# First four heads' parts stored ahead of the others; batch 1's third part spread over the lead's units of maxima

## The chip, the cores and the metric

The kernel runs on one core of a Trainium2 chip. The metric is device time in microseconds of the whole program, from its start to its end. One core has TensorE (matrix products), VectorE, ScalarE and GpSimd for elementwise work, SyncE which here only issues transfers, and 16 DMA engines that carry them. TensorE's weight loads and products are told apart in the rows as PEld and PE, the transfers issued by SyncE as SPq.

## What is computed

Four layers over x of 2 batches, 1024 tokens, 128 channels. Cut to their cores:

```python
x = _layernorm(x + retention(x))      # L0_attn: 8 heads, rotary, decayed causal scores, gate silu(g)
x = _layernorm(x + L0_ffn(x))         # below
x = _layernorm(x + attention16(x))    # L1_attn: 16 heads of 8, two masked corners
x = _layernorm(x + x @ (ternary(W) * scale).T)

def L0_ffn(x):
    x = x + mla_attention(rmsnorm(x))  # 16 heads of 8, causal
    return x + moe(rmsnorm(x))         # 4 experts, top 1

def mla_attention(x):
    q = x @ Wq.T                       # rotated
    latent = layernorm(x @ Wdkv.T)     # 64 wide
    k, v = latent @ Wuk.T, latent @ Wuv.T   # k rotated
    return softmax(causal(q @ k.T / sqrt(8))) @ v @ Wo.T
```

The change bears on the hand-over from the first layer, the retention, to `mla_attention`.

## The kernel before

Everything is written by hand: each engine has its own instruction stream, and counting semaphores join them. The rows of x are 16 tiles of 128 tokens, 8 for each batch.

**Retention** runs a loop over the 16 tiles, numbered 0 to 15, a few steps of each tile late. The norm, projections and rotation of `mla_attention` are done for groups of four tiles, which I call parts 0 to 3 (two for each batch). Parts 0 and 1 (batch 0) are made inside this loop. Part 2 and 3 (batch 1) are made later, part 2 at the place of this change. q and k of a part are split into three bf16 pieces, so that bf16 products give float32 accuracy, and stored to DRAM (`store_parts`, L1163) as seven copies in the order in which products need them. From there they are loaded again as *stacks*: one stack (`load_stack`, L1182) holds four heads, with (head dimension, piece) along the partitions, 56 rows for even heads and 56 for odd ones. The stored rows are 128 partitions: 16 heads of 8, so heads 0 to 3 are partitions 0 to 31. `store_parts(0, 0)` is called for batch 0 of the first attention; its first half of columns (part 0) is stored at 197 us, its second (part 1) as soon as the last piece is made.

**Attention** works on blocks m: a group of four heads and one half of the queries. For each block the row maxima of the scores are found first, in *units of maxima* `A (u, x)`: TensorE makes 128 queries by up to 512 keys for two heads into a pair of PSUM banks, VectorE reduces it. When a block's units are done, `M` transposes its maxima, ScalarE copies them and GpSimd's `split` cuts them in three bf16 pieces and sends them by three small transfers into the query stack. Only then can the block's scores `S (s, x)` be made on TensorE, already less their maxima; ScalarE takes exp of them and `V` multiplies by the values. Units of maxima run ahead of the scores by a *lead* of 8 to 12 units, so the first 8 units (steps -8 to -1) have no scores beside them.

**What sets the order.** `order()` builds one list of all steps from tables of (step, what), and each engine goes through the same list and takes its share of each entry. So a step that waits holds up all later entries of that engine. Steps whose PSUM is taken from the common ring (`RINGED`: A, M, T0, Q, QS, lat and others) get bank pairs alternately, banks 2 and 3, then 0 and 1; entry r waits until entry r-2 has been emptied. The steps at one number stand behind that number's units of maxima, the split last (L1123 sorts them so).

Names of this place:
- `D16a`, `D16b`, `D16c`, `D17a`, `D17b`: last steps of the retention's last tile, 15. On TensorE D16a is its gate product (L485), D16b the projection of tile 14 (L495), D16c the turn of tile 15 (L504), D17a the projection of tile 15 (L495). ScalarE's share of D17a is `affine` (L521, 8 instructions), VectorE's `gated` (L542).
- `hn`, `T0`, `Q`, `QS`, `lat`, `ls`, `q_rot` of part 2: scaling (ScalarE L447); transposes (TensorE L1494, copied by ScalarE L1782); the query product and its swapped twin (L1499, copied at L1788); the latent product (L1510, copied at L1799); the latent's statistics (VectorE L468 and L471) and after them the reciprocal root on GpSimd (`latents_rooted`, L453 and L383 to L387); the rotation of the queries (GpSimd L460 to L462).
- `ln3`: root of the last part's norm on GpSimd (L1318, then L383 to L434).
- `warm`: products into an unused bank, of 128x512 (L1427), whose result nobody reads.
- Units of maxima: products at L1477 and L1487, reductions at L1930 (two heads) and L1927 (narrow units). Scores: L1557 and L1566. M: L1529, its copy L1818. Split: L1331 to L1334, its transfers L1341.

## Time and profile before

| | |
|---|---|
| median of 3 runs | 1020.18 us (1018.56 to 1020.27) |
| profiled execution, its own time | 1024.54 us |
| its span, first to last instruction | 1022.1 us |
| TensorE's mean granted clock | 0.957 |
| busy: TensorE, VectorE, ScalarE, GpSimd | 87%, 75%, 64%, 38% |
| transfers | 52.51 MB, mean 51 GB/s |

All times in the rows are microseconds from the span's start, in this one execution. A row of the order of time gives start, duration, engine, line, operation, tiles and count; a merged row counts the instructions and its duration goes from the first to the last. What stands in brackets is how long the engine was idle before, and what released it. The chain of waits is followed back from the last instruction: at each step to what released it. PEclk is TensorE's granted clock: 1.00 is 2.4 GHz, 0.50 is 1.2 GHz.

### The profile page before, as it was taken

To read this page: it belongs to the slowest core of one execution; us is meant where nothing else is said; L and a number is where in the kernel's file an instruction comes from. 1 tells how busy PE (TensorE), PEld (TensorE's weight loads), DVE (VectorE), ACT (ScalarE), POOL (GpSimd) and SP (SyncE) were. 2 spreads that over 40 slices of the span, in tenths; PEclk is the share of its full clock that TensorE was granted. 3 is DMA by queue.
4 is the path that set the end of the run, shared out by engine and by line. 5 is a ranking of instruction groups with operands and counts; after the bars stand their busy time and mean duration, and the time that the engine had idled before them with its cause. 6 is when DMAs were issued, how large, how long until landed. Compare 5 with 4: busy or idle time off the path is not lost.

```text
span 1022.1 us, 22793 instructions
## 1 busy us (share of the span) xinstructions
PE 890.6 (87%) x9065; PEld 445.1 (44%) x9070; DVE 762.3 (75%) x1155; ACT 655.0 (64%) x1285; POOL 392.0 (38%) x607
## 2 busy tenths in 40 slices
PE   5999999998877889988798778879988999999983
PEld 3778677777632343333472322216422222222232
DVE  3667766856487678886458498776889999999954
ACT  2554655655526678774446547765767988898981
POOL 2755757878332552134345111352432111111240
PEclk8999999999899999997799899989999999999997
DMA  8000000200501034111420601032206100000000
GB/s 294 1 1 2 1 1 2 73 2 1 150 1 41 21 128 138 38 43 52 122 74 2 199 21 38 5 92 85 75 2 187 32 20 20 21 20 2 5 23 21
DMA packets 49405, 52.51 MB, mean 51 GB/s; under 512 B 8874, under 2 KB 40618, under 8 KB 49140
## 3 DMA queue, kind: packets, MB, share of 16 engines
q1 hardware_dynamic: 45012, 48.12, 15.5%
q0 software_dynamic: 4288, 2.94, 1.1%
q8 instruction: 72, 1.18, 0.5%
q14 instruction: 33, 0.27, 0.1%
HBM read 32.37 MB, written 19.68 MB: 51 GB/s over the span
## 4 chain that ended last, share of the span: by engine, by line
PE 50%; DVE 27%; ACT 7%; issue 6%; DMA 4%; POOL 3%; SPq 2%; another core or an unknown queue 1%; DVEq 0%; ACTq 0%; POOLq 0%
DVE arena L1930 19%; PE banks L1592 10%; PE banks L1557 7%; PE banks L1477 5%; ACT arena L1750 3%; PE banks L740 3%; PE banks L485 3%; PE banks L495 2%; PE banks L1667 2%; PE banks L1675 2%; PE banks L673 2%; DMA arena<-arena 1%; PE banks L735 1%; PE banks L699 1%; ACT arena L521 1%
## 5 line engine op out<-in xcount | busy, mean ns | idle before, releaser
L1930 DVE TENSOR_REDUCE arena<-banks 128x2 f32<-128x1024 f32 (+1 forms) x384 | 440.9, 1198 | 65.4 <-PE banks L1477 33.0
L1750 ACT ACTIVATE arena<-banks 128x512 f32<-128x512 f32 (+1 forms) x768 | 409.4, 587 | 120.9 <-PE banks L1557 77.7
L1592 PE MATMUL banks<-arena 128*9 128x256 f32 (+1 forms) x3328 | 257.0, 385 | 6.8 <-ACT arena L1763 4.6
L1557 PE MATMUL banks<-arena 61*128 61x512 bf16 (+4 forms) x896 | 167.5, 373 | 33.9 <-ACT arena L1750 23.7
L1477 PE MATMUL banks<-arena 56*128 56x512 bf16 (+3 forms) x896 | 165.2, 371 | 29.1 <-DVE arena L1930 22.1
L1557 PEld LDWEIGHTS banks<-arena 61*128 61x128 bf16 (+1 forms) x896 | 44.7, 93 | 194.5 <-ACT arena L1750 160.8
L1331 POOL CAST arena<-arena 16x128 bf16<-16x128 f32 x32 | 9.0, 282 | 301.0 <-ACT arena L1818 292.3
L1592 PEld LDWEIGHTS banks<-arena 128*9 128x9 f32 x3328 | 51.6, 89 | 133.0 <-issue 86.7
L1477 PEld LDWEIGHTS banks<-arena 56*128 56x128 bf16 x896 | 45.2, 95 | 54.6 <-DVE arena L1930 40.9
L383 POOL TENSOR_TENSOR arena<-arena 128x8 f32<-128x8 f32 (+1 forms) x35 | 51.3, 1466 | 30.2 <-DVE arena L2094 27.8
L1341 POOL DMA_DIRECT2D arena<-arena x96 | 55.2, 579 | 10.7 <-POOL arena L1334 9.2
L521 ACT ACTIVATE arena<-banks,arena 128x128 f32<-128x128 f32 x128 | 46.4, 477 | 0.5 <-PE banks L504 0.5
L1371 POOL DMA_INDIRECT expert_rows<-arena x22 | 21.4, 972 | 54.9 <-DVE arena L2026 54.9
L1927 DVE TENSOR_REDUCE arena<-banks 128x4 f32<-128x1024 f32 (+1 forms) x32 | 30.4, 954 | 16.2 <-PE banks L1487 13.5
L511 ACT ACTIVATE arena<-banks 128x1024 f32<-128x1024 f32 x16 | 16.4, 1022 | 39.9 <-PE banks L740 39.9
L554 DVE TENSOR_TENSOR arena<-banks,arena 128x128 f32<-128x128 f32 x16 | 4.7, 291 | 47.0 <-PE banks L495 47.0
L1746 ACT ACTIVATE arena<-banks 128x512 f32<-128x512 f32 (+1 forms) x64 | 27.9, 490 | 17.2 <-PE banks L1566 16.9
L529 ACT ACTIVATE arena<-banks 128x1024 f32<-128x1024 f32 x16 | 16.4, 1026 | 33.9 <-PE banks L485 32.5
L767 DVE TENSOR_TENSOR arena<-banks,arena 128x1024 f32<-128x1024 f32 x16 | 19.6, 1223 | 24.0 <-PE banks L673 23.9
L485 PE MATMUL banks<-arena 128*128 128x128 f32 x256 | 33.9, 287 | 2.6 <-DVE arena L770 2.6
L673 PE MATMUL banks<-arena 128*128 128x512 f32 x64 | 32.8, 637 | 1.7 <-DMA arena<-c_gk 1.7
L866 POOL TENSOR_TENSOR arena<-arena 128x512 f32<-128x512 f32 x16 | 25.3, 1578 | 22.5 <-DVE arena L770 22.5
(239 smaller groups left out, 1463.5 us busy)
## 6 DMA issues: line engine op xcount, KB each, us to landing
arena<-k_products SPq DMA_DIRECT2D x32, 224.0 KB
arena<-q_products SPq DMA_DIRECT2D x64, 112.0 KB
q_products<-arena SPq DMA_DIRECT2D x16, 384.0 KB, 3.3
k_products<-arena SPq DMA_DIRECT2D x16, 384.0 KB, 3.8
arena<-e_w SPq DMA_DIRECT2D x22, 256.0 KB
arena<-arena POOLq DMA_DIRECT2D x96, 4.0 KB, 1.7
sorted_rows<-c_pads SPq DMA_DIRECT2D x2, 709.5 KB, 8.6
arena<-sorted_rows SPq DMA_DIRECT2D x4, 258.0 KB, 3.1
```

Source lines behind the costliest of these rows:

```text
L383: link(eng.tensor_tensor(y, v, epst[:, 1:2].to_broadcast(list(v.shape)), ALU.pow))
L485: ins = nc.tensor.matmul(bank(s // 4)[:, (s % 4) * P:(s % 4 + 1) * P], wg[:, s * P:(s + 1) * P], XT[:, i, :], start=True, stop=True)
L521: ins = nc.scalar.activation(ga[:, s, :], bank(4 + s // 4)[:, (s % 4) * P:(s % 4 + 1) * P], ACT.Identity, scale=gn[:, 0, s:s + 1], bias=gn ...
L673: ins = nc.tensor.matmul(bank(c), XT[:, n + 1, :], wqk[:, c * 512:(c + 1) * 512], start=True, stop=True)
L740: ins = nc.tensor.matmul(bank(2 + s // 4)[:, (s % 4) * P:(s % 4 + 1) * P], sm[:, s, :], vv[n % 2][:, s, :], start=first, stop=True, skip_g ...
L1341: g_.dma_start(rows, nmp[k % 2][:, i, :]).then_inc(mrow[k % 2], 16)
L1477: ins = nc.tensor.matmul(bank(first + par)[:, at:at + hi - lo], Qs[k_][rows, qc, y, qo:qo + P], Ks[k_][rows, y, lo:hi], start=True, stop=n ...
L1557: ins = nc.tensor.matmul(bank(S_BANK + (use + par) % SCORES)[:, at:at + C - o], Ks[n % NS][rows, y, kt * P:(kt + 1) * P], Qs[n % NS][rows, ...
L1592: ins = nc.tensor.matmul(PS[h * VROWS:h * VROWS + VW, AV_BANK, o:end], V[:, b, kt, HG * g + h, :], Pr[u % PROBS][:, h, o:end], start=(kt = ...
L1750: s_.activation(Pr[s % PROBS][:, 2 * x + par, o:C], scores[:, o:C], ACT.Exp) \
L1927: v_.tensor_reduce(of, two_banks.rearrange("p r (y e) -> p r y e", y=2)[:, :, :, 0:width], AX.X, ALU.max).then_inc(ring_dve, 1)
L1930: v_.tensor_reduce(of[:, :, x], two_banks[:, :, 0:width], AX.X, ALU.max).then_inc(ring_dve, 1)
```

## The change

Two things. First, `store_parts` takes a range of partitions. For batch 0 of the first attention it is called for partitions 0 to 31 (heads 0 to 3) before the first stack is loaded, and for partitions 32 to 127 after it, ahead of the second stack's load. The counts that stored parts are waited for with go up by one group of transfers. Second, the steps of part 2 from T0 to q_rot, which all stood at step -9, ahead of the first unit of maxima, stand at steps -8 to -3, and `("warm", 6)` at step -7 is gone.

```diff
--- before.py
+++ after.py
@@ -415,7 +415,7 @@
         def stored_wait(eng, w, i):
 
             if i >= 2:
-                eng.wait_ge(part_stored[w][i % 2], 16 * PART_DMAS[w] * (i // 2))
+                eng.wait_ge(part_stored[w][i % 2], 16 * PART_DMAS[w] * (i // 2 + 1))
 
         def first_of(m):
 
@@ -1065,9 +1065,9 @@
 
         def batch1_projections():
 
-            at = [(-9, e) for e in (("D16a", 15), ("warm", 8), ("D16b", 15), ("hn", 2), ("T0", 2), ("D16c", 15), ("Q", 2), ("QS", 2), ("lat", 2),
-                                    ("ls", 2), ("q_rot", 2))]
-            at += [(-8, ("warm", 2)), (-7, ("warm", 6)), (-7, ("D17a", 15)), (-6, ("D17b", 15)), (-2, ("ln3", 3)),
+            at = [(-9, e) for e in (("D16a", 15), ("warm", 8), ("D16b", 15), ("hn", 2), ("D16c", 15))]
+            at += [(-8, ("T0", 2)), (-8, ("warm", 2)), (-7, ("D17a", 15)), (-7, ("Q", 2)), (-6, ("D17b", 15)), (-6, ("QS", 2)),
+                   (-5, ("lat", 2)), (-4, ("ls", 2)), (-3, ("q_rot", 2)), (-2, ("ln3", 3)),
                    (1, ("q_part0", 2)), (5, ("ln", 2)), (6, ("KL", 2)), (6, ("xs3", 3)), (6, ("q_rem", 2)), (7, ("K", 2)),
                    (7, ("q_part1", 2)), (8, ("KS", 2)), (8, ("k_rot", 2)), (8, ("q_part2", 2)), (9, ("V0", 2)),
                    (10, ("hn", 3)), (11, ("T0", 3)), (12, ("Q", 3)), (13, ("QS", 3)), (14, ("lat", 3)), (15, ("ls", 3)),
@@ -1160,7 +1160,7 @@
 
             @block.sync
             def _(sp):
-                def store_parts(l, b):
+                def store_parts(l, b, lanes=slice(0, P), turn=0):
                     for c in range(2):
                         cols = slice(c * C, (c + 1) * C)
                         item = l * 4 + 2 * b + c
@@ -1168,16 +1168,18 @@
 
                         sp.wait_ge(pj["q_part2"], item + 1)
                         for i in range(2):
-                            sp.dma_start(q_dram[l, b, :, 3 * i:3 * i + 3, cols],
-                                         q[:, i:i + 1, :].to_broadcast([P, 3, C])).then_inc(part_stored[0][c], 16)
-                        sp.dma_start(q_dram[l, b, :, 6:7, cols], q[:, 2:3, :]).then_inc(part_stored[0][c], 16)
+                            sp.dma_start(q_dram[l, b, lanes, 3 * i:3 * i + 3, cols],
+                                         q[lanes, i:i + 1, :].to_broadcast([lanes.stop - lanes.start, 3, C])) \
+                              .then_inc(part_stored[0][c], 16)
+                        sp.dma_start(q_dram[l, b, lanes, 6:7, cols], q[lanes, 2:3, :]).then_inc(part_stored[0][c], 16)
                         sp.wait_ge(pj["k_part2"], item + 1)
                         for i in range(2):
-                            sp.dma_start(k_dram[l, b, :, 3 * i:3 * i + 3, cols], k).then_inc(part_stored[1][c], 16)
-                        sp.dma_start(k_dram[l, b, :, 6:7, cols], k[:, 0:1, :]).then_inc(part_stored[1][c], 16)
+                            sp.dma_start(k_dram[l, b, lanes, 3 * i:3 * i + 3, cols], k[lanes]) \
+                              .then_inc(part_stored[1][c], 16)
+                        sp.dma_start(k_dram[l, b, lanes, 6:7, cols], k[lanes, 0:1, :]).then_inc(part_stored[1][c], 16)
                     for w in range(2):
                         for c in range(2):
-                            sp.wait_ge(part_stored[w][c], 16 * PART_DMAS[w] * (l * B + b + 1))
+                            sp.wait_ge(part_stored[w][c], 16 * PART_DMAS[w] * (l * B + b + 1 + (l + b + turn > 0)))
 
                 def load_stack(n, part):
                     l, b, g, k = n // (B * NG), n // NG % B, n % NG, n % NS
@@ -1254,12 +1256,13 @@
                     for i in range(W1S, SORTED):
                         load_w1(b, i, steer)
 
-                store_parts(0, 0)
+                store_parts(0, 0, slice(0, HG * AD))
                 sp.wait_ge(k_rotated, NTILE)
                 sp.wait_ge(rot_ready, NTILE)
                 sp.wait_ge(qkT_done, NTILE)
                 load_all(0)
                 load_ones(sp, 0)
+                store_parts(0, 0, slice(HG * AD, P), 1)
                 load_all(1)
                 load_ones(sp, 1)
                 sp.wait_ge(g_done, NTILE)
```

On **TensorE**, from the last tile's steps into the lead, before (L1494 is T0, L504 the turn of tile 15, L1499 Q and QS, L1510 lat, L1477 and L1487 a unit of maxima):

```order
L495 MATMUL banks<-arena 128x128 x8
L1494 MATMUL banks<-arena 128x128 x4
L504 MATMUL banks<-arena 128x128 x8
L1499 MATMUL banks<-arena 128x512 x2
L1510 MATMUL banks<-arena 128x64 x4
L1477 MATMUL banks<-arena 128x512 x2
L1487 MATMUL banks<-arena 128x64 x4
L1477 MATMUL banks<-arena 128x512 x2
L1487 MATMUL banks<-arena 128x64 x4
L1427 MATMUL banks<-arena 128x512 x2
L1477 MATMUL banks<-arena 128x384 x2
```

and now (lines are three higher: L1480 and L1490 are a unit, L1497 is T0, L1430 the fillers, L495 the projection of tile 15; Q, L1502, follows the last row shown):

```order
L495 MATMUL banks<-arena 128x128 x8
L504 MATMUL banks<-arena 128x128 x8
L1480 MATMUL banks<-arena 128x512 x2
L1490 MATMUL banks<-arena 128x64 x4
L1480 MATMUL banks<-arena 128x512 x2
L1490 MATMUL banks<-arena 128x64 x4
L1497 MATMUL banks<-arena 128x128 x4
L1430 MATMUL banks<-arena 128x512 x2
L1480 MATMUL banks<-arena 128x384 x2
L1490 MATMUL banks<-arena 128x64 x4
L1480 MATMUL banks<-arena 128x384 x2
L1490 MATMUL banks<-arena 128x64 x4
```

T0 went behind the first two units, Q behind the last tile's projection; QS and lat follow one unit each later.

On **ScalarE** at the same place, before (L1782 is T0's copy, L521 the affine, L1788 and L1799 the copies of Q, QS and lat, L1818 that of the maxima):

```order
L529 ACTIVATE arena<-banks 128x1024
L447 ACTIVATE arena<-arena 128x128 x4
L1782 ACTIVATE arena<-banks,arena 128x512
L1788 ACTIVATE arena<-banks 128x512 x2
L1799 ACTIVATE arena<-banks 128x256
L521 ACTIVATE arena<-banks,arena 128x128 x8
L1818 ACTIVATE arena<-banks 16x128
```

and now:

```order
L529 ACTIVATE arena<-banks 128x1024
L447 ACTIVATE arena<-arena 128x128 x4
L1785 ACTIVATE arena<-banks,arena 128x512
L521 ACTIVATE arena<-banks,arena 128x128 x8
L1791 ACTIVATE arena<-banks 128x512 x2
L1802 ACTIVATE arena<-banks 128x256
L1821 ACTIVATE arena<-banks 16x128
```

The affine of the last tile (the second L521) went ahead of the copies of Q, QS and lat; T0's copy still stands directly ahead of it.

On **GpSimd**, behind the latent's root, whose end is L387, before (L460 to L462 are q_rot, L1331 to L1341 the first split and its transfers, L1318 the start of ln3):

```order
L387 TENSOR_TENSOR arena<-arena 128x4
L460 TENSOR_TENSOR arena<-arena 128x512
L461 TENSOR_TENSOR arena<-arena 128x512
L462 TENSOR_TENSOR arena<-arena 128x512
L1331 CAST arena<-arena 16x128
L1332 TENSOR_TENSOR arena<-arena 16x128
L1333 CAST arena<-arena 16x128
L1334 TENSOR_TENSOR arena<-arena 16x128
L1341 DMA arena<-arena 2x8x128 x3
```

and now (L1334 to L1344 are the split, L1321 the start of ln3):

```order
L387 TENSOR_TENSOR arena<-arena 128x4
L1334 CAST arena<-arena 16x128
L1335 TENSOR_TENSOR arena<-arena 16x128
L1336 CAST arena<-arena 16x128
L1337 TENSOR_TENSOR arena<-arena 16x128
L1344 DMA arena<-arena 2x8x128 x3
L460 TENSOR_TENSOR arena<-arena 128x512
L461 TENSOR_TENSOR arena<-arena 128x512
L462 TENSOR_TENSOR arena<-arena 128x512
```

The root of part 2 now stands directly ahead of the first split, and q_rot between it and ln3. On VectorE the statistics (L468, L471) went from ahead of the first unit's reduction to behind A(4,1)'s.

## Rows read from the trace of the kernel before

**Rows 1.** Chain of waits, 255 to 320 us: start, duration, what.
```profile
264.85 3.51 DMA k_products<-arena
...
308.39 3.73 DMA arena<-arena
```

**Rows 2.** Busy time, PEclk, DMA share and GB/s, in stretches of 1 us.
```profile
265.00:266.00 1.00, 0.92 (x8) 0.92 (x9) 0.02 (x1) 0.88 (x1) 0.76 (x4) 1.00 0.97 337
...
272.00:273.00 1.00, 0.00 (x0) 0.00 (x0) 0.61 (x4) 1.00 (x4) 0.00 (x0) 1.00 0.97 215
...
280.00:281.00 1.00, 1.00 (x6) 1.00 (x6) 0.00 (x0) 0.00 (x0) 0.81 (x1) 0.50 0.00 0
...
282.00:283.00 1.00, 1.00 (x19) 0.80 (x17) 0.00 (x0) 0.00 (x0) 0.00 (x0) 1.00 0.00 0
```

**Rows 3.** Order of time, SyncE's queue: start, duration, engine, line, operation.
```profile
261.57 0.89 SPq L1171 DMA_DIRECT2D q_products<-arena  x2
```

**Rows 4.** Order of time, TensorE; in brackets the idle time before.
```profile
265.08 2.05 PE L495 MATMUL banks<-arena 128*128 128x128 f32 x16 [0.75 <-DVE arena L542]
267.45 0.63 PE L1494 MATMUL banks<-arena 128*128 128x128 f32 x4 [0.32 <-ACT arena L447]
...
268.95 1.96 PE L1499 MATMUL banks<-arena 128*128 128x512 f32 x4
270.74 1.10 PE L1510 MATMUL banks<-arena 128*128 128x64 f32 x8
273.98 0.39 PE L1477 MATMUL banks<-arena 56*128 56x512 bf16 x2 [2.14 <-DMA arena<-q_products]
...
277.42 2.74 PE L1427 MATMUL banks<-arena 128*128 128x512 bf16 x6
279.95 2.66 PE L495 MATMUL banks<-arena 128*128 128x128 f32 x16
...
282.99 1.04 PE L1427 MATMUL banks<-arena 128*128 128x512 bf16 x3
...
294.78 0.39 PE L1557 MATMUL banks<-arena 59*128 59x512 bf16 x2
```

**Rows 5.** Order of time, VectorE.
```profile
272.36 0.61 DVE L468 BATCH_NORM_STATS2 arena<-arena 128x6 f32<-128x64 f32 x4 [3.93 <-ACT arena L1799]
...
274.47 4.09 DVE L1930 TENSOR_REDUCE arena<-banks 128x2 f32<-128x1024 f32 x4 [1.08 <-PE banks L1487]
278.47 1.22 DVE L542 TENSOR_TENSOR arena<-arena 128x1024 f32<-128x1024 f32 x1
283.10 1.23 DVE L1927 TENSOR_REDUCE arena<-banks 128x4 f32<-128x1024 f32 x1 [3.42 <-PE banks L1487]
...
286.40 2.35 DVE L1930 TENSOR_REDUCE arena<-banks 128x2 f32<-128x1024 f32 x2
```

**Rows 6.** Order of time, ScalarE.
```profile
268.12 0.69 ACT L1782 ACTIVATE arena<-banks,arena 128x512 f32<-128x512 f32 x1 [0.81 <-PE banks L1494]
...
272.16 2.90 ACT L521 ACTIVATE arena<-banks,arena 128x128 f32<-128x128 f32 x8
```

**Rows 7.** Order of time, GpSimd.
```profile
273.47 0.23 POOL L453 TENSOR_SCALAR arena<-arena 128x4 f32<-128x4 f32 x1 [7.04 <-DVE arena L471]
...
275.76 0.20 POOL L387 TENSOR_TENSOR arena<-arena 128x4 f32<-128x4 f32 x1
...
278.61 2.20 POOL L462 TENSOR_TENSOR arena<-arena 128x512 f32<-128x512 f32 x1
288.32 0.28 POOL L1331 CAST arena<-arena 16x128 bf16<-16x128 f32 x1 [7.51 <-ACT arena L1818]
...
297.68 0.20 POOL L387 TENSOR_TENSOR arena<-arena 128x4 f32<-128x4 f32 x1
```

**Rows 8.** GpSimd's transfers of the first row of maxima, 286 to 300 us.
```profile
L1341 POOL DMA_DIRECT2D arena<-arena x3: 560/566/814, 290.2 to 291.6; - x3
...
DMA to landing us min/median/max: 1.7/1.7/1.9
```

## The prediction

> **What bounds the kernel now.** The change touches one place of the run: the hand-over from the retention phase to the attention lead, 260 to 312 us. I read the chain of waits first, then the order of time of each engine there. The chain shows which transfers are waited for: the last store of batch 0's parts, 3.51 us, and the last transfer of the second row of maxima, 3.73 us [rows 1]. SyncE's queue says why the first one is on the path: the stores of the second half start at 261.57 [rows 3], the last lands at 264.85 + 3.51 = 268.36, and only then may the load of the first stack be issued. TensorE waits for that stack 2.14 us and starts the first unit of maxima, A(0,0), at 273.98 [rows 4]. In the 2 to 10 us before it, TensorE, ScalarE and VectorE do T0, Q, QS, lat and ls of batch 1's third part, under cover of this transfer [rows 4 to 6]. From 274.47 on VectorE sets the pace with its reductions of about 1.17 us, but for a gap of 3.42 us before 283.10, where it waits for A(2,0) behind the last tile's projection [rows 4, 5]. S(0,0), the first product of scores, runs at 294.78 [rows 4]. It needs the row of maxima that GpSimd splits from 288.32 and whose last transfer is issued at 291.6 and lands 1.7 us later, at 293.3 [rows 7, 8]. So this row is there 1.5 us before it is wanted. Behind S(0,0) the run is one chain of equal steps to the end, and what S(0,0) loses or gains the end does.
>
> I follow four marks through the change: A(0,0) starts, A(2,0)'s reduction starts (283.10), A(4,1)'s reduction ends (286.40 + 2.35 = 288.75, [rows 5]), S(0,0) starts.
>
> **Part 1: the store of the first four heads goes ahead.** Of the 1.8 MB that goes out between 262.5 and 268, a quarter is left in front of the load. The stores move 337 GB/s while they run [rows 2], so the quarter is 1.3 us of transfer, less than its six issues take. Six issues of about 0.45 us (the first two took 0.89, [rows 3]) put the last at 263.8. From issue to landing such a store takes between 1.7 us (the smallest transfer here, [rows 8]) and 3.51 us (the last store, with a queue ahead of it, [rows 1]). I take 1.8, since little is queued: it lands at 265.6 instead of 268.36. The loads are the same, so A(0,0) comes **2.75 us earlier** (bounds 2.9 and 1.05), at 271.2. TensorE is free by then: the turn of the last tile ends near 268.8, since T0 no longer stands before it.
> One row speaks against the full rate: the load into 56 partitions at a time moves 215 GB/s where the store of 128 moves 337 [rows 2]. The Trainium skill, "SBUF — State Buffer", section "Door 1: The DMA port swizzle", says that partitions 0 to 31 reach 8 of the 16 ports; by it the quarter would move at about half the rate, an estimate of 2.7 us of transfer, and A(0,0) would come about 0.7 us later than I say. The trace has no transfer of 32 partitions.
> The rest of the store, 96 partitions of both halves, 12 issues and some 2.7 MB, now stands between the first and the second stack's load. At the same rate it is 8 us, to about 279, and the second stack is in by 285; it is first read by units of maxima behind S(0,0). Cost nothing. The waits raised by one DMA group in the later stores and copies are met long before.
>
> **Part 2: what moves into the lead.** The engines' work is the same but for 6 fillers less on TensorE (2.74 us at half clock, [rows 4]). What counts is the order in each queue.
> From A(0,0) to A(2,0) it was 283.10 - 273.98 = 9.12 us. Now T0 stands in the ring of bank pairs behind A(0,1) and takes A(0,0)'s pair, so it starts when that is reduced; and ScalarE has T0's copy ahead of the last tile's affine, which before was under way at 272.16 [rows 6]. The gate product, the projection, then Q, and only then A(2,0) follow. The chain: A(0,0) 0.49, its reduction 1.2, T0 0.63 at full and 1.26 at half clock, copy 0.69, affine 2.90, gate 1.22, projection 2.05 at full clock (265.08) and 4.1 at half, Q 1.0 (half of 1.96), A(2,0) 0.55, hand-overs 0.4 in all [rows 4 to 6]. The clock is at 0.50 (1.2 GHz) at 280 and at 1.00 (2.4 GHz) at 282 [rows 2]; it fell after TensorE's wait for the stack and came back after it had been busy without a gap from 277.4. The wait remains, the six fillers that began that busy time are gone, and it now begins with the projection; so I take T0 at half and the projection at 3.2, between its two ends. Sum 12.9, **3.8 us more** (bounds 2.0 and 4.7).
> From A(2,0) to the end of A(4,1) it was 5.65 us, with VectorE nearly always busy. Now TensorE is the longer: 4 fillers 1.04 (the row counts 3, one record is missing), QS 1.0, A(3,0) 0.45, 4 fillers 1.04, lat 1.1, A(4,0) 0.4, then two reductions 2.35: 7.38 [rows 4, 5]. **1.7 us more** (1.4 to 2.0).
> From there to S(0,0) it was 6.03 us. Now ls stands next on VectorE, 1.11 us from its start to GpSimd's (272.36 to 273.47), and GpSimd's queue has the roots for it ahead of the split of the maxima: 273.47 to 275.96, 2.49 us [rows 5, 7]. Then the split and its transfers, 5.0 as above, and 0.15 of hand-overs: 8.75 us, **2.7 us more** (2.4 to 3.1). VectorE's own road to S(0,0) is shorter (ls adds 1.1, and half of that goes into its wait for A(5,0)), so the row of maxima, which had 1.5 us in hand, ends last, and TensorE waits some 2 us for it.
> q_rot moves behind the split's transfers on GpSimd, and pushes ln3, which ended at 297.88. q_rot took 4.85 us, 275.96 to 280.81, and the second split's last transfer was issued at 308.39 [rows 1, 7]: even shifted by 1.4 and 4.85 us against S(0,0), GpSimd is free before its four casts. Cost nothing; the cover is about 1 to 2 us.
> Behind S(0,0) the next wait, for the second row of maxima, keeps its shape, since split, load of the third stack and units all move together: 0.
>
> **Sum.** -2.75 + 3.8 + 1.7 + 2.7 = +5.45 us. Against the profiled run, 1024.54 us (span 1022.1), that is 1030.0; this run is 4.4 above the median of the three, 1020.18, and the same difference on the median gives **1025.6 us**. With all terms at their ends it is +2.9 to +8.75.
>
> **Rivals.**
> Faster: the steps that were moved fall into TensorE's and VectorE's idle time in the lead (the 3.42 us before A(2,0), the 6 fillers' 2.74), as the change would have it. Then the earlier stack is kept, 2.9, and only ls is new on VectorE, 1.1: -1.8, 1018.4 us. For it speaks the 3.42 us of idle [rows 5]. It decides at the affine: for A(2,0) by 281.1 the gate has to begin by 276.1 and the affine by 273.1. T0's copy, which stands ahead of it in ScalarE's queue, can't begin before 271.2 + 0.49 + 1.2 + 0.63 = 273.5. 0.14.
> No change: TensorE's clock never falls, since work comes sooner behind a shorter wait, and the row of maxima comes in time because VectorE and GpSimd are quicker than summed. Then -2.9 + 2.0 + 1.4 and 0.6 for ls: +1.1, 1021.3 us. Against it: the wait of 2.4 us before A(0,0) is no shorter than the one behind which the clock fell [rows 2, 4]. 0.18.
> Slower still: the quarter store is held back by its few partitions and lands 3.5 us after its last issue [rows 1], and GpSimd is late for the second split because its products stretch as the one at 278.61 did, 2.20 us for 1.3 [rows 7]. Then 1.5 and 1 to 2 more: +8, 1028.2 us. 0.10.
> That the rows of maxima do not bind and only VectorE's road does: +3.4, 1023.6; it is within my forecast's case.
>
> **The numbers.** Forecast's case (row of maxima last, or VectorE's road, +2.1 to +8) 0.58, slower still 0.10, no change 0.18, faster 0.14. A difference under 0.2% (2 us) can't be told from none here. Faster by more 0.14, within 0.18, slower 0.68. The range leaves out half of the faster case and the far end of the slower one: 1018.8 to 1028.8 us.
>
> **What would show it.** Right: the load of the first stack issued near 265.8 and A(0,0) near 271; T0's copy directly ahead of the last affine, near 274; VectorE idle for some 5 us before A(2,0), at about 284; the roots directly ahead of the first split, which begins near 295; S(0,0) near 300, behind an idle of TensorE that ends with a transfer of the row of maxima. Wrong: S(0,0) before 294.8; A(2,0) before 282, with the clock at 1.00 all through; a store of 32 partitions that lands as late as one of 128; or a wait elsewhere in the kernel that takes the shift up.

## The result, and the profile after

The changed kernel takes 1026.81 us (median of 10 runs, 1023.74 to 1028.43), the kernel before on the same chip 1019.97 (10 runs, 1016.19 to 1022.02). The ratio is 1.0064, with a 95% interval of 1.0049 to 1.0078: **slower by 6.5 us**, between 5.0 and 8.0. The forecast was +5.45. A second set of runs of the same kernel, further down, gives 1.0056 (1.0033 to 1.0079).

The profiled execution of after took 1027.36 us (span 1025.7, mean granted clock 0.953), that of before 1024.54 (span 1022.1, 0.957). These two differ by only 2.8 us. The last section shows the main reason: before's profiled run holds a stray stall, worth some 3.7 us at the end, that after's does not. So the two spans can't be subtracted, and I read the one place that was changed instead.

The chain of waits of after, 255 to 330 us: start, duration, what.

```profile
264.97 1.70 DMA k_products<-arena
268.11 3.84 DMA arena<-q_products
...
273.92 1.13 PE banks L1497 x4
275.66 2.91 ACT arena L521 x8
278.59 1.24 DVE arena L542
279.87 3.74 PE banks L495 x16
283.61 0.86 PE banks L1502 x2
...
289.26 2.36 DVE arena L1933 x2
291.61 0.52 DVE arena L468 x4
...
298.33 1.66 DMA arena<-arena
...
313.84 4.56 DMA arena<-arena
```

This is the forecast's chain, in its order: the store that is waited for (1.70 us where before's was 3.51, [rows 1]), the load, T0 (L1497) with its copy, the last tile's affine (L521), the gate (L542), the projection (L495), Q (L1502); then the two reductions of A(4,1), ls (L468), and the row of maxima, whose transfer (298.33, 1.66 us) was in no chain before at this place [rows 1]. The order of time of after, SyncE's queue: the stores' first issue, and the load of the first stack.

```profile
262.74 0.78 SPq L1171 DMA_DIRECT2D q_products<-arena  x2
...
266.87 0.75 SPq L1198 DMA_DIRECT2D arena<-k_products  x2
```

TensorE, in brackets the idle time before and what ended it: A(0,0) and S(0,0).

```profile
272.08 0.39 PE L1480 MATMUL banks<-arena 56*128 56x512 bf16 x2 [2.09 <-DMA arena<-q_products]
...
300.12 0.39 PE L1560 MATMUL banks<-arena 59*128 59x512 bf16 x2 [2.10 <-DMA arena<-arena]
```

ScalarE: T0's copy and the last affine.

```profile
275.08 0.69 ACT L1785 ACTIVATE arena<-banks,arena 128x512 f32<-128x512 f32 x1 [6.61 <-PE banks L1497]
275.66 2.90 ACT L521 ACTIVATE arena<-banks,arena 128x128 f32<-128x128 f32 x8
```

VectorE: A(2,0)'s first reduction.

```profile
284.96 1.23 DVE L1930 TENSOR_REDUCE arena<-banks 128x4 f32<-128x1024 f32 x1 [5.14 <-PE banks L1490]
```

The second half's stores began 1.17 us later in this execution than in before's (262.74 against 261.57). The profiles of the kernels below put that start anywhere from 260.68 to 262.74, so it is drift of an execution and no effect of the change. All distances below are therefore counted from the first issue of these stores, which I call q. The marks are those of the prediction, and a last one, S(4,0), the first unit of scores that needs the second row of maxima:

| | before | after | difference | forecast |
|---|---|---|---|---|
| q to A(0,0) | 12.41 | 9.34 | -3.07 | -2.75 |
| A(0,0) to A(2,0)'s reduction | 9.12 | 12.88 | +3.76 | +3.8 |
| A(2,0)'s reduction to A(4,1)'s end | 5.65 | 6.66 | +1.01 | +1.7 |
| A(4,1)'s end to S(0,0) | 6.03 | 8.50 | +2.47 | +2.7 |
| sum at S(0,0) | 33.21 | 37.38 | +4.17 | +5.45 |
| S(0,0) to S(4,0) | 17.39 | 18.33 | +0.94 | 0 |

VectorE's idle time before A(2,0) rose from 3.42 us [rows 5] to 5.14, ScalarE stood idle 6.61 us and then did T0's copy ahead of the affine, and TensorE waits 2.10 us at S(0,0) for the transfer of the row of maxima. Before, it did not wait there [rows 4].

The clock, in the windows of after (columns as in [rows 2]):

```profile
265.00:266.00 1.00, 0.50 (x3) 0.00 (x1) 1.00 (x1) 0.00 (x0) 1.00 (x1) 1.00 0.79 192
280.00:281.00 1.00, 1.00 (x5) 1.00 (x6) 0.00 (x0) 0.00 (x0) 0.00 (x0) 0.50 0.99 283
283.00:284.00 1.00, 1.00 (x6) 0.64 (x4) 0.00 (x0) 0.00 (x0) 0.00 (x0) 0.78 0.00 0
```

The first is the quarter store of 32 partitions, 192 GB/s. The other two say that the granted clock was 0.50 (1.2 GHz) in the projection and came back to 1.00 (2.4 GHz) within 283 to 284, at the projection's end.

### The profile page after: what moved, and what is told of

Its sections match the earlier page's. It is cut to its first block, busy times and chain, and to the rows that moved or that the text cites. A ratio compares the mean times of both kernels' runs of the same rounds, so it can differ in the third digit from the quotient of the medians.

```text
span 1025.7 us, 22800 instructions
## 1 busy us (share of the span) xinstructions
PE 891.0 (87%) x9064; PEld 447.1 (44%) x9064; DVE 762.6 (74%) x1155; ACT 654.9 (64%) x1285; POOL 390.0 (38%) x607
## 4 chain that ended last, share of the span: by engine, by line
PE 50%; DVE 26%; ACT 7%; issue 7%; POOL 4%; DMA 4%; SPq 1%; DVEq 0%; ACTq 0%; POOLq 0%
DVE arena L1933 18%; PE banks L1595 10%; PE banks L1560 7%; PE banks L1480 5%; ACT arena L1753 3%; PE banks L740 3%; PE banks L485 3%; PE banks L495 2%; PE banks L1670 2%; PE banks L1678 2%; PE banks L673 2%; ACT arena L521 1%; PE banks L735 1%; DMA arena<-arena 1%; PE banks L699 1%
## 5 line engine op out<-in xcount | busy, mean ns | idle before, releaser
L1480 PE MATMUL banks<-arena 56*128 56x512 bf16 (+3 forms) x896 | 165.3, 372 | 28.8 <-DVE arena L1933 22.9
L1334 POOL CAST arena<-arena 16x128 bf16<-16x128 f32 x32 | 8.9, 279 | 284.9 <-ACT arena L1821 281.0
L1480 PEld LDWEIGHTS banks<-arena 56*128 56x128 bf16 x896 | 45.2, 96 | 55.1 <-DVE arena L1933 42.5
L1344 POOL DMA_DIRECT2D arena<-arena x96 | 55.0, 577 | 10.7 <-POOL arena L1337 9.2
L521 ACT ACTIVATE arena<-banks,arena 128x128 f32<-128x128 f32 x128 | 46.4, 477 | 0.5 <-PE banks L504 0.5
L485 PE MATMUL banks<-arena 128*128 128x128 f32 x256 | 34.1, 289 | 2.6 <-DVE arena L770 2.6
L495 PE MATMUL banks<-arena 128*128 128x128 f32 x256 | 33.1, 284 | 3.8 <-DVE arena L542 3.8
```

The source lines that it names most:

```text
L485: ins = nc.tensor.matmul(bank(s // 4)[:, (s % 4) * P:(s % 4 + 1) * P], wg[:, s * P:(s + 1) * P], XT[:, i, :], start=True, stop=True)
L495: ins = nc.tensor.matmul(bank(7)[:, 0:P], uu[:, s, :], wo[:, s, :], start=(s == 0), stop=(s == RH - 1))
L521: ins = nc.scalar.activation(ga[:, s, :], bank(4 + s // 4)[:, (s % 4) * P:(s % 4 + 1) * P], ACT.Identity, scale=gn[:, 0, s:s + 1], bias=gn ...
L1344: g_.dma_start(rows, nmp[k % 2][:, i, :]).then_inc(mrow[k % 2], 16)
L1480: ins = nc.tensor.matmul(bank(first + par)[:, at:at + hi - lo], Qs[k_][rows, qc, y, qo:qo + P], Ks[k_][rows, y, lo:hi], start=True, stop=n ...
```

## The experiments

The first question was which of the two parts costs the time; then, which of the moved steps. Each kernel's time is compared with runs of before on the same chip. For "part 1 alone", "part 2 alone", "ls behind the split" and "T0 back" that is 1021.08 us (29 runs); for "fillers back", "the three together", "ls behind the gate" and "after, again" it is 1022.7 (35); for "the same, again" and "gate ahead" 1019.46 (23). After ran beside its own ten runs of before and again beside the second of these sets, so for the first set a difference from after is a difference of two ratios from two chips. The ratio is worked out over all runs, so it need not equal that of the medians. Marks are from each kernel's own profile, in us from q.

| kernel | A(0,0) | A(2,0) | S(0,0) | S(4,0) | projection takes | median | ratio (95%) |
|---|---|---|---|---|---|---|---|
| before | 12.41 | 21.53 | 33.21 | 50.60 | 2.66 | 1019.97 | 1 |
| after | 9.34 | 22.22 | 37.38 | 55.71 | 3.74 | 1026.81 | 1.0064 (1.0049 to 1.0078) |
| after, again | 9.27 | 22.11 | 37.30 | 54.53 | 3.71 | 1029.15 | 1.0056 (1.0033 to 1.0079) |
| part 1 alone | 10.20 | 19.51 | 31.18 | 48.49 | 1.97 | 1020.70 | 0.9980 (0.9960 to 1.0000) |
| part 2 alone | 12.32 | 25.18 | 40.36 | 58.50 | 3.46 | 1027.49 | 1.0052 (1.0036 to 1.0068) |
| ls behind the split | 9.31 | 23.40 | 36.99 | 53.81 | 3.78 | 1023.25 | 1.0017 (1.0000 to 1.0034) |
| T0 back | 9.31 | 21.12 | 36.28 | 53.76 | 3.78 | 1022.67 | 1.0010 (0.9994 to 1.0025) |
| fillers back | 9.43 | 20.88 | 36.04 | 53.61 | 2.05 | 1026.54 | 1.0035 (1.0017 to 1.0052) |
| the three together | 9.21 | 18.44 | 32.02 | 50.15 | 2.05 | 1023.13 | 0.9997 (0.9978 to 1.0016) |
| ls behind the gate | 10.20 | 18.57 | 30.37 | 48.69 | 2.05 | 1020.49 | 0.9970 (0.9952 to 0.9988) |
| the same, again | 10.19 | 18.56 | 30.35 | 48.79 | 2.05 | 1017.95 | 0.9983 (0.9968 to 0.9999) |
| gate ahead | 10.19 | 17.32 | 30.18 | 47.44 | 2.03 | 1017.80 | 0.9977 (0.9963 to 0.9992) |

### Part 1 alone

After's store with before's table of steps:

```
-            at = [... ("hn", 2), ("D16c", 15)]
-            at += [(-8, ("T0", 2)), (-8, ("warm", 2)), (-7, ("D17a", 15)), (-7, ("Q", 2)), ...
+            at = [... ("hn", 2), ("T0", 2), ("D16c", 15), ("Q", 2), ("QS", 2), ("lat", 2), ("ls", 2), ("q_rot", 2)]
+            at += [(-8, ("warm", 2)), (-7, ("warm", 6)), (-7, ("D17a", 15)), (-6, ("D17b", 15)), (-2, ("ln3", 3)), ...
```

> Only part 1 of the change: the first four heads' parts are stored ahead, the table of steps is that of before. My theory: the stack lands near 271, but TensorE is then still at the latent product (to 272) and VectorE at its statistics (to 273.4), which stood under the cover of the transfer. So the first reduction of maxima begins at about 273.5 instead of 274.47, and the end moves by -1 us, ratio 0.999. Rival: all of the transfer's gain arrives, -2.8 us, ratio 0.997. A second rival: the stores of the other heads, now between the two stacks, hold something up: +1 us or more.

Measured: 2.0 us faster (0 to 4.1), S(0,0) 2.0 us sooner. A(0,0) came at 10.20 and not at 9.3, because here the third part's steps still stand in front of it on TensorE. VectorE's order of time:

```profile
272.92 0.61 DVE L468 BATCH_NORM_STATS2 arena<-arena 128x6 f32<-128x64 f32 x4 [3.93 <-ACT arena L1802]
273.56 0.38 DVE L471 BATCH_NORM_AGGREGATE arena<-arena 128x2 f32<-128x6 f32 x4
273.85 2.33 DVE L1933 TENSOR_REDUCE arena<-banks 128x2 f32<-128x1024 f32 x2
```

The first reductions stand directly behind ls: with the stack early, ls is what holds up VectorE. Part 1 is sound and worth about 2 us, by the ratio and at S(0,0); the two medians differ by only 0.4. All of the loss is in part 2.

### Part 2 alone

Before's store with after's table (the reverse of the diff above).

> Only part 2: the steps from T0 to q_rot spread over the lead, no six fillers, but the whole store ahead of the first stack as before. My theory: A(0,0) at 274 as before, then the after kernel's own distances: 12.9 us to A(2,0) instead of 9.1, 6.7 instead of 5.65 to the end of A(4,1), 8.5 instead of 6.0 to the first scores, and 0.9 for the clock behind them: +8.2 us, ratio 1.008. Rival: the two parts need each other, and with the stack late the moved steps cost little: +3 us or less.

Measured: 5.3 us slower (3.7 to 6.9), S(0,0) 7.15 us later. TensorE's order of time, the projection and S(0,0):

```profile
281.87 3.46 PE L495 MATMUL banks<-arena 128*128 128x128 f32 x16 [3.01 <-DVE arena L542]
...
301.86 0.60 PE L1557 MATMUL banks<-arena 59*128 59x512 bf16 x2 [2.10 <-DMA arena<-arena]
```

The same picture as in after, 3 us later. S(4,0) came 7.9 us later, about as expected, but the time grew by less than the 8.2 that I had put on it. At S(0,0) the parts add up, nearly: -2.03 + 7.15 = +5.12 against +4.17 measured for both. In the time they give -2.0 + 5.3 = +3.3, and both together +6.5 and +5.7. The intervals of the three nearly bridge that; what they don't stays open.

### ls behind the first split

One entry of after's table, which puts the third part's ls one step later, so that GpSimd's roots don't stand ahead of the first row of maxima:

```
-                   (-5, ("lat", 2)), (-4, ("ls", 2)), (-3, ("q_rot", 2)), ...
+                   (-5, ("lat", 2)), (-3, ("ls", 2)), (-3, ("q_rot", 2)), ...
```

> The changed kernel with the latent's statistics and root (ls) one step later, at step -3, so that GpSimd splits the first row of maxima before it takes the roots. My theory (the row of maxima, queued behind the roots, ends last before the first scores): the first split begins about 2.5 us earlier and S(0,0) comes when VectorE's reductions allow, 6.6 us behind the end of A(4,1) instead of 8.5: 1.9 us less than the changed kernel, +4.5 us against before, ratio 1.0045. Rival: VectorE's lengthened road or the clock sets it, and the roots only fill GpSimd's idle time: as the changed kernel, 1.0064.

Measured: +1.7 us against before (0 to 3.5), that is 4.8 us less than after. GpSimd's order of time:

```profile
291.50 0.28 POOL L1334 CAST arena<-arena 16x128 bf16<-16x128 f32 x1 [24.79 <-ACT arena L1821]
...
295.79 0.23 POOL L453 TENSOR_SCALAR arena<-arena 128x4 f32<-128x4 f32 x1 [0.44 <-DVE arena L471]
```

TensorE's, the two halves of Q, and S(0,0):

```profile
282.56 1.92 PE L1502 MATMUL banks<-arena 128*128 128x512 f32 x2
...
286.03 1.02 PE L1502 MATMUL banks<-arena 128*128 128x512 f32 x2
...
298.86 0.39 PE L1560 MATMUL banks<-arena 59*128 59x512 bf16 x2
```

The split now runs ahead of the roots, S(0,0) has no wait in brackets, and the distance from A(2,0) to S(0,0) is 13.59 instead of 15.16: 1.6 us of the last stretch, from A(4,1)'s end to S(0,0), is the order of GpSimd's queue (expected were 1.9). In this profile Q's first half, and the unit A(2,0) behind it, also ran at the half clock (Q 1.92 us; its second half, the same work, took 1.02), and A(2,0) came 1.2 us later than in after, which is why S(0,0) shows only 0.4 us of gain. What the clock does to a neighbour is of the size of the effect.

### T0 back in the turn of the last tile

```
-            at = [... ("hn", 2), ("D16c", 15)]
-            at += [(-8, ("T0", 2)), (-8, ("warm", 2)), ...
+            at = [... ("hn", 2), ("T0", 2), ("D16c", 15)]
+            at += [(-8, ("warm", 2)), ...
```

> The changed kernel with T0 of part 2 back at step -9, ahead of the turn of the last tile; Q, QS, lat, ls and q_rot stay in the lead. My theory (T0 in the bank ring and its copy ahead of the affine lengthen the way to the last projection): the affine begins near 270, the reductions of the first four units follow without a gap and the projection starts near 278 instead of 279.9: A(0,0) to A(2,0) 11 us instead of 12.9, so 1.9 us less than the changed kernel, +4.6 us against before, ratio 1.0045. Rival: the way to A(2,0) is set by TensorE's clock alone: the gap moves and the total stays at 1.0064.

Measured: +1.0 us (-0.6 to +2.6), 5.5 less than after. ScalarE's order of time:

```profile
269.44 2.90 ACT L521 ACTIVATE arena<-banks,arena 128x128 f32<-128x128 f32 x8 [0.18 <-PE banks L504]
```

TensorE's:

```profile
277.16 3.78 PE L495 MATMUL banks<-arena 128*128 128x128 f32 x16 [2.25 <-DVE arena L542]
```

Counted from q, the affine starts 5.5 us sooner than in after (7.42 against 12.92), but the projection only 2.0 us sooner (15.14 against 17.13): the gate is next, and it stands on VectorE behind the reductions of the first four units. TensorE still waits 2.25 us for it, the clock still falls, and the projection still takes 3.78. A(0,0) to A(2,0) is 11.81 us, where 11 was expected and after has 12.88.

### The six fillers back

```
-            at += [(-8, ("T0", 2)), (-8, ("warm", 2)), (-7, ("D17a", 15)), ...
+            at += [(-8, ("T0", 2)), (-8, ("warm", 2)), (-7, ("warm", 6)), (-7, ("D17a", 15)), ...
```

> The changed kernel with the six fillers of step -7 put back ahead of the last tile's projection, all else as changed. They fit into TensorE's idle time of 3.0 us there. My theory (the clock, not the wait, makes the projection 3.74 us long): the clock is back at full when the projection begins or soon after, it takes 2.0 to 2.7 us, and A(0,0) to A(2,0) is 11.4 instead of 12.9 us: 1.4 us less than the changed kernel, ratio to before 1.005. Rival: the clock does not come back in time, or the fillers only shift its fall: no difference from the changed kernel, 1.0064.

Measured: +3.6 us (1.7 to 5.3). TensorE's order of time:

```profile
275.08 2.28 PE L1430 MATMUL banks<-arena 128*128 128x512 bf16 x6
...
278.16 2.05 PE L495 MATMUL banks<-arena 128*128 128x128 f32 x16 [0.80 <-DVE arena L542]
```

The windows, columns as in [rows 2]:

```profile
276.00:277.00 1.00, 1.00 (x5) 0.31 (x3) 0.71 (x2) 0.84 (x3) 0.00 (x0) 0.62 0.87 254
...
278.00:279.00 1.00, 0.84 (x7) 0.84 (x8) 0.10 (x1) 0.00 (x0) 0.00 (x0) 1.00 0.96 281
```

The fillers sit in TensorE's wait for the gate. The clock comes back within 276 to 277 instead of 283 to 284, and the projection takes 2.05 us instead of 3.74. A(2,0) is 1.34 us sooner. Six products that compute nothing were worth 1.3 us to this hand-over.

### The three together

After's table with the three edits above at once.

> The changed kernel with three things put right at once: T0 back at step -9, the latent's statistics and root behind the first split, the six fillers back. If these three and the moved products are all of the loss, the marks are: A(0,0) 3.1 us earlier, 9.3 us from there to A(2,0), 13.6 from there to the first scores instead of 11.7: in all 1 us less than before, ratio 0.999. Rival: something else of the change costs (the second store between the stacks, or q_rot's new place): 1.003 or more.

Measured: 0.3 us faster than before (2.2 faster to 1.6 slower), 6.0 less than after on the same chip; S(0,0) 5.36 us sooner than after and 1.2 sooner than before. TensorE's order of time:

```profile
276.56 2.05 PE L495 MATMUL banks<-arena 128*128 128x128 f32 x16 [1.06 <-DVE arena L542]
...
293.55 0.39 PE L1560 MATMUL banks<-arena 59*128 59x512 bf16 x2
```

VectorE's, A(4,0) and A(4,1):

```profile
284.26 2.36 DVE L1933 TENSOR_REDUCE arena<-banks 128x2 f32<-128x1024 f32 x2 [0.92 <-PE banks L1480]
```

One by one the edits gave 0.39 + 1.10 + 1.34 = 2.83 us at S(0,0), together 5.36. T0's return alone leads to a projection at half clock; the fillers' return alone leaves the affine late. Only with both does A(2,0) come 3.8 us sooner. Part of this can be the one execution: here the granted clock was 1.00 in every window from 262 to 298, while in the profiles of the three single returns it fell to 0.50 at 269 to 273. In the time it is the other way round: the single returns gave 4.8, 5.5 and 2.1 us against after, the first two by ratios from another chip, and together only 6.0. So that the three are causes is shown, by the marks and by the time of all three; the share of each is not.

Part 1's gain is still in this kernel, so its equal is "part 1 alone" and not before. Against that, what is left of the change (Q, QS, lat, ls and q_rot spread over the lead) brings A(0,0) and A(2,0) 1.0 and 1.1 us sooner. Then it costs 1.0 us from A(2,0) to A(4,1)'s end (6.65 against 5.65), where QS, lat and their turns stand between the units on TensorE, and 0.9 us from there to S(0,0) (6.93 against 6.02), where ls is new on VectorE. S(0,0) comes 0.84 us later, S(4,0) 1.7. The ratios, 0.9997 (0.9978 to 1.0016) and 0.9980 (0.9960 to 1.0000), do not tell the two apart. The moved products gain nothing that shows, and probably cost a little.

### ls and q_rot behind the gate product

This goes the other way: before's table, and out of it only the two steps that part 1 alone had shown in VectorE's way, put behind the last tile's gate:

```
+            at = [... ("hn", 2), ("T0", 2), ("D16c", 15), ("Q", 2), ("QS", 2), ("lat", 2)]
+            at += [(-8, ("warm", 2)), (-7, ("warm", 6)), (-7, ("D17a", 15)), (-7, ("ls", 2)), (-7, ("q_rot", 2)), (-6, ("D17b", 15)), ...
```

> The early store with T0, Q, QS and lat where they were before, but the latent's statistics (ls) and q_rot behind the last tile's gate, where VectorE waits 3.4 us for the projection. My theory (in the kernel with the early store alone, VectorE's first reduction waited for these statistics, to 273.85): the first reduction begins 1 us earlier, right behind A(0,0), the root and the rotation lie in GpSimd's idle time before the first split: ratio 0.997, 1 us less than with the early store alone. Rival: the affine of the last tile, 2.9 us behind the copy of lat, or the fillers set the projection, and nothing is gained: 0.998 as there.

Measured: 3.1 us faster than before (1.2 to 4.9). Run again with the last kernel:

> The kernel ls_behind_gate once more, beside gate_ahead on the same chip: 0.997 again if its gain of 3 us is real, within 0.995 to 0.999. If the early store alone had all of the gain and the new place of ls had none, it would be 0.998 or above.

Measured: 1.7 us faster (0.1 to 3.3). VectorE's order of time in the second profile:

```profile
273.09 4.08 DVE L1932 TENSOR_REDUCE arena<-banks 128x2 f32<-128x1024 f32 x4 [3.90 <-PE banks L1489]
...
278.23 0.60 DVE L468 BATCH_NORM_STATS2 arena<-arena 128x6 f32<-128x64 f32 x4
...
280.90 1.23 DVE L1929 TENSOR_REDUCE arena<-banks 128x4 f32<-128x1024 f32 x1 [1.67 <-PE banks L1489]
```

The reductions start as soon as A(0,0) is there, ls lies in the gap before A(2,0), and of that gap 1.67 us is left, where before had 3.42 [rows 5] and part 1 alone 2.60. S(0,0) is 2.85 us sooner than before in both profiles. But 2.03 of that is part 1 alone, and at S(4,0) nothing is left of the other 0.8 (48.69 and 48.79 against 48.49). The ratios 0.9970 and 0.9983 lie on both sides of part 1 alone's 0.9980, and by the bound that the second expectation set (0.998 or above if ls's new place gains nothing) a gain of the new place is not shown.

### The gate ahead of the reductions

The same, and the affine and the gate of the last tile are issued one step sooner, behind the first two reductions instead of the first four, apart from the projection:

```
-            at += [(-8, ("warm", 2)), ...
+            at += [(-8, ("D17g", 15)), (-8, ("warm", 2)), ...
...
-                    elif kind == "D17a":
+                    elif kind == "D17g":
```

(the second pair on ScalarE and on VectorE; TensorE's projection stays at D17a)

> The kernel ls_behind_gate with one more step moved: the gate of the last tile (ScalarE's affine, VectorE's product) stands behind the first two reductions of maxima instead of the first four, the projection on TensorE stays where it is. My theory (VectorE waits about 3 us for A(2,0) because the projection starts only when four reductions and the gate are through): the projection starts behind the fillers, near 277.5, while VectorE reduces the third and fourth unit, VectorE's wait before A(2,0) falls from 2.7 to about 1 us, and A(0,0) to A(2,0) from 8.4 to 7 us: 1.4 us less, ratio to before 0.996. Rival: the affine ends only at 275.9, the gate waits for it, and what is gained behind it is lost before it: 0.997 as ls_behind_gate.

Measured: 2.3 us faster than before (0.8 to 3.8), no clear step beyond the kernel without it, 1.7 (0.1 to 3.3) on the same chip. VectorE's order of time:

```profile
275.26 1.23 DVE L542 TENSOR_TENSOR arena<-arena 128x1024 f32<-128x1024 f32 x1 [0.39 <-ACT arena L521]
```

TensorE's: the projection, and one of the units ahead of S(0,0).

```profile
276.56 2.03 PE L495 MATMUL banks<-arena 128*128 128x128 f32 x16
...
286.48 0.61 PE L1479 MATMUL banks<-arena 56*128 56x512 bf16 x2
```

A(0,0) to A(2,0) fell from 8.37 to 7.13 us as expected, but the next stretch, to S(0,0), grew from 11.79 to 12.86. The chain of waits puts some 0.6 us of that on the units that ran at half clock in this profile (0.61 us where 0.39 is usual) and 0.4 on a small step of VectorE (L1939, 0.67 us where it took 0.29). This one profile does not tell whether that belongs to the kernel. A gain ahead of a wait is not yet a gain behind it.

### After, again

To see how much of the distances is chance of one execution, after ran once more, unchanged.

> The changed kernel itself, on the same chip as the three others, so that they can be set against it. 1.0064 as before, between 1.005 and 1.008. Its profile shows whether the full length of the wait before the first scores (2.1 us, for a transfer of the row of maxima) and the half clock behind it, 301 to 307, belong to the kernel or to one execution: I expect both again, and the wait for the second row of maxima, 4.56 us from issue to landing, within 0.5 us.

Measured: +5.7 us (3.4 to 8.1). The marks up to S(0,0) came again within 0.11 us (9.27, 22.11, 37.30); only S(0,0) to S(4,0) moved, from 18.33 to 17.23. Over the profiles of these kernels this distance lies between 16.8 and 18.4 us, with no order in it that follows an edit. The wait before S(0,0) came again (2.12 us), and so did the half clock behind it; the wait for the second row of maxima did not: 3.50 us, a miss of the expected 4.56 within 0.5. In "part 1 alone" it is 4.77, so it is no mark of the change.

## Why the prediction was right, step by step

**The store and the load.** Forecast: landed 4.0 us after the first issue. Measured: 262.74 to 264.97 + 1.70 = 266.67, 3.93 us; the load followed at 266.87. A(0,0) came 3.07 us sooner, not 2.75. By the Trainium skill, "SBUF — State Buffer", section "Door 1: The DMA port swizzle", partitions 0 to 31 reach 8 of the 16 ports; the forecast's estimate from it was half the rate and 0.7 us more. The window shows a lower rate: 192 GB/s at a DMA share of 0.79, where the store of 128 partitions has 337 at 0.97 [rows 2]. That is 0.57 as it stands, and 0.70 per full share (243 against 347). No delay from it shows: the last transfer landed 1.70 us after its issue, as the smallest ones do [rows 8], and the six issues (2.66 us, 262.74 to 265.40) set the pace.

**From A(0,0) to A(2,0).** Forecast 12.9, measured 12.88, by the forecast's own chain. Its two choices about the clock held: T0 at half (1.13 us; I took 1.26), the projection between its ends (3.74; I took 3.2, of 2.05 to 4.1). That the sum is right to 0.02 us is luck: from the projection's start to Q's, 279.87 to 283.44, it was 3.57 us, 0.37 more than I took, and the other links together were 0.40 less, since they too were durations laid end to end, as below. "Part 2 alone", "T0 back" and "the fillers back" show the parts of it separately.

**From A(2,0) to A(4,1)'s end.** Forecast 7.38, measured 6.66. The mechanism was right, TensorE is the longer there, but the term was mis-sized by 0.7 us. I had added the durations of grouped rows end to end, and they overlap. TensorE's order of time of after:

```profile
283.44 1.02 PE L1502 MATMUL banks<-arena 128*128 128x512 f32 x2
...
284.85 1.04 PE L1430 MATMUL banks<-arena 128*128 128x512 bf16 x4
285.72 1.02 PE L1502 MATMUL banks<-arena 128*128 128x512 f32 x2
286.68 0.23 PE L1480 MATMUL banks<-arena 56*128 56x128 bf16 x2
...
287.02 1.04 PE L1430 MATMUL banks<-arena 128*128 128x512 bf16 x4
287.89 1.00 PE L1513 MATMUL banks<-arena 128*128 128x64 f32 x8
288.82 0.39 PE L1480 MATMUL banks<-arena 56*128 56x512 bf16 x2
```

From start to start the rows from 284.85 on are 0.87, 0.96, 0.34, 0.87 and 0.93 us, where I had taken 1.04, 1.0, 0.45, 1.04 and 1.1: together 0.66 us, and 0.11 more because the first fillers start before A(2,0)'s reduction does. Each row's duration holds the end of its last product, under which the next row has begun.

**From A(4,1)'s end to S(0,0).** Forecast 8.75, measured 8.50; the row of maxima ends last, TensorE waits 2.10 us for it (forecast: some 2). "ls behind the split" took 1.6 us of it away.

**Nothing further on.** The second row of maxima is waited for 4.56 us where it was 3.73 [rows 1], but S(0,0) to S(4,0) does not tell +0.94 (first profile) from -0.16 (second). The forecast's zero stands as far as S(4,0). The rest of the store, 12 issues from 270.69 on, held up no unit: part 1 alone shows no loss behind it. It did take longer than forecast: the load of the second stack, which waits for it, was issued at 283.24 and lasted to 289, where I had it in by 285.

**The sum.** At S(0,0) it was +4.17 and +4.09 in the two profiles against +5.45: two terms that erred by -0.3 and -0.7, and a third by -0.2. The time came out at +6.5 and +5.7. So the forecast stood nearer to the time than its steps deserve: at S(4,0) the traces carry +5.1 and +3.9, and 1 to 2 us up to the ratios' differences are missing. Two other kernels show such a remainder from the other side: "T0 back" and "ls behind the split" gained 5.5 and 4.8 us in time against after, but 2.0 and 1.9 at S(4,0) of their one profile.

The prediction's premise was that behind S(0,0) the end does what S(0,0) does. The single executions don't bear that out. A mark far behind is the first of GpSimd's indirect transfers that sort batch 1's tokens by expert. GpSimd's order of time, before:

```profile
664.92 1.09 POOL L1358 DMA_INDIRECT sorted_rows<-arena  x1 [7.29 <-DVE arena L1987]
```

after:

```profile
672.36 1.09 POOL L1361 DMA_INDIRECT sorted_rows<-arena  x1 [7.30 <-DVE arena L1990]
```

after, again:

```profile
665.90 1.10 POOL L1361 DMA_INDIRECT sorted_rows<-arena  x1 [7.29 <-DVE arena L1990]
```

From q that is 403.35, 409.62 and 403.89 us: the first profile of after is 6.3 us behind before there, the second only 0.5, although it was 3.9 behind at S(4,0). "Part 1 alone", 2.1 ahead at S(4,0), is level with before. The distance from S(4,0) to this mark goes with TensorE's mean granted clock over it. In four profiles with 0.95 (after again among them) it is 349.4 to 351.7 us, in three with 0.94 351.7 to 352.8, in five with 0.93 (before, after, part 1 alone among them) 352.8 to 355.7. The times of the runs do likewise: in the second set of after the shortest, 1023.96 us, had a mean clock of 0.960 and the longest, 1032.64, 0.950. So a single profile can't carry a difference of a few microseconds to the end, and most of what it loses or gains on the way goes with the clock of that execution. That the missing 1 to 2 us are clock too fits the means over the runs (0.955 in both sets of after, 0.960 in the 35 runs of before beside the second), but what of this clock the change itself brings about is not shown.

**The rivals.** "Faster" was decided where the prediction put it: the affine would have had to begin by 273.1, T0's copy could not begin before 273.5. Measured: copy at 275.08, affine at 275.66 (273.9 and 274.5 with the 1.17 us of drift taken off). "No change" needed a clock that doesn't fall; it was 0.50 in both profiles of after. "Slower still" did not happen: the store was not held back, and GpSimd was not late. The reason for the likeliest case, that T0 stands ahead of the affine and six fillers are gone from the wait, is shown by their return. With both, and ls behind the split, the kernel is level with before, and 0.84 us behind "part 1 alone" at S(0,0).

## What to carry to other kernels

An idle stretch on one engine is no free place for a step that another engine's next link has to wait behind: here T0 was moved into a lead in which VectorE had 3.42 us of idle, and its copy then stood ahead of the affine that the idle time was waiting for. Before steps are moved into a gap, write down what ends the gap and put them behind that in every queue they issue to; "ls behind the gate" does so and is 2 to 3 us faster than before, where the change was 6.5 slower, though most or all of that gain is the early store. Set each kernel against the one that differs from it by the step in question, not against before. And look at fillers in a wait before they are taken out: with six of them back, the clock was at 1.00 when the projection began, and without them at 0.50.

## What the runs showed of the hardware

**A stray stall, worth 3 to 4 us.** Before's profiled execution has one far away from the change. The waits of before, 665 to 682 us (engine, buffer, line, what was waited for, us in total, times, longest):

```profile
ACT arena L1750 <- remote: 5.4, 2, 3.5
```

Its chain of waits there:

```profile
670.07 3.49 another core or an unknown queue
...
674.67 1.88 another core or an unknown queue
```

ScalarE stood still 3.5 and then 1.9 us, TensorE 3.3 and 0.9, while GpSimd was in the indirect transfers of the sort, and no releaser is in the records (there is no other core in this program). The same is among the waits of the second profile of after, at the same place:

```profile
ACT arena L1753 <- remote: 4.5, 2, 2.4
```

It is in 5 of 12 profiles (before, after again, fillers back, the three together, ls behind the gate), and absent in the other 7, the first of after among them. It follows no edit. Its price can be read: from the first indirect transfer of this sort to the end of the span it is 356.9 to 357.4 us in the five, and 353.0 to 353.8 in the seven. With these some 3.7 us the two profiled times, which differ by 2.8, come to 6.5, where the medians differ by 6.8. The prediction had placed its sum on the median with the difference of before's run (4.4 us), which came out well. The stall alone does not set how a profiled run lies to its median: the second of after has it and lies 4.8 us below. What causes the stall is open, and also how often it comes in runs without a profile.

**The price of the clock at one projection.** The same 16 products took 2.05 us at a granted clock of 1.00, 3.74 at 0.50 with the return inside it, and 2.66 where the return came earlier [rows 4]. That is 1.7 us in one hand-over. Whether a neighbour such as Q falls to the low level too changed from profile to profile. So did whether the clock falls here at all: it stayed at 1.00 through the projection in "the three together", "ls behind the gate" and "gate ahead".
